# Two projections of the next block moved forward in the cross stage of a three-layer decoder kernel

## What is computed

```python
# linear attention, chunks of 32 keys (here as masked scores over each sequence of 64)
q, k, v = silu(rms(x) @ Wq.T), silu(rms(x) @ Wk.T), silu(rms(x) @ Wv.T)
g = sigmoid(rms(x) @ Wg.T)
x1 = layernorm(x + (linear_attention(q, k, v) * g) @ Wp.T)
# cross attention over a latent context of 64 channels, 16 heads
scores = (rope(q_big(x1)) @ W_qr) . (rope(ctx) @ W_kr)
ctx_c  = softmax(scores) @ rope(ctx)
x2 = layernorm(x1 + (ctx_c @ w_kc_kv) @ Wo.T)
# 32 experts of 96 hidden units, the best 8 of each token, weighted
out = layernorm(x2 + sum_e c_e * (silu(x2 @ Wg_e.T) * (x2 @ Wu_e.T)) @ Wd_e.T)
```

## Time and profile before

| | |
|---|---|
| Median of 3 runs | 843.66 us (843.52 to 843.76) |
| The profiled execution, device time | 843.54 us |
| Its span in the profile | 841.7 us |
| TensorE (PE) matmuls busy | 821.1 us, 98% |
| TensorE weight loads (PEld) busy | 658.0 us, 78% |
| VectorE (DVE) busy | 631.0 us, 75% |
| ScalarE (ACT) busy | 290.7 us, 35% |
| GpSimd (POOL) busy | 180.8 us, 21% |

### The profile page before, as it was taken

One profiled execution on the slowest core, in us unless ns is written; L12 is line 12 of the kernel. 1 busy time (PEld: TensorE's weight loads), 2 busy tenths in 40 slices (PEclk: granted clock), 3 DMA queues, 4 the chain that ended last, 5 costly groups with the idle time before them and its releaser, 6 DMA issues.

```text
span 841.7 us, 16104 instructions
## 1 busy us (share of the span) xinstructions
PE 821.1 (98%) x6386; PEld 658.0 (78%) x6386; DVE 631.0 (75%) x1392; ACT 290.7 (35%) x532; POOL 180.8 (21%) x156
## 2 busy tenths in 40 slices
PE   8999999999999999999999999999999999999996
PEld 6977677776887768776777788888888888888885
DVE  5587698899889998887957966666665666576576
ACT  5431263204432145303544423342323333232242
POOL 3046500663006630176312102100000000000121
PEclk9999999999999999999999999999999999999998
DMA  9300000100001000010220042102012021000001
GB/s 349 145 26 2 3 2 4 60 2 5 2 14 51 3 5 2 17 66 5 81 62 26 1 139 89 70 1 70 31 45 69 0 93 36 26 1 1 0 34 67
DMA packets 13092, 35.86 MB, mean 43 GB/s; under 512 B 1504, under 2 KB 2784, under 8 KB 12640
## 3 DMA queue, kind: packets, MB, share of 16 engines
q1 hardware_dynamic: 13024, 34.92, 12.1%
HBM read 30.26 MB, written 2.36 MB: 39 GB/s over the span
## 4 chain that ended last, share of the span: by engine, by line
PE 49%; DVE 2%; issue 1%; ACT 0%; POOL 0%; ACTq 0%; DVEq 0%
PE ps L259 15%; PE ps L260 15%; PE ps L261 15%; PE ps L1711 2%; PE ps L642 1%; PE ps L1702 0%; PE ps L1677 0%; PE ps L645 0%; PE ps L670 0%; DVE h_lo L374 0%; POOL roped L824 0%; ACT roped L979 0%; DVE su L543 0%; PE ps L1698 0%; PE ps L1542 0%
## 5 line engine op out<-in xcount | busy, mean ns | idle before, releaser
L824 POOL TENSOR_TENSOR roped<-prod 128x512 f32<-128x512 f32 x96 | 121.3, 1289 | 226.2 <-DVE prod L1175 226.1
L543 DVE TENSOR_TENSOR su<-sg,ps 128x512 f32<-128x512 f32 x96 | 66.0, 687 | 119.5 <-PE ps L261 117.3
L259 PE MATMUL ps<-y_hi,f_hi 128*128 128x512 f32 x384 | 150.8, 393 | 0.0
L261 PE MATMUL ps<-y_hi,f_lo 128*128 128x512 f32 x384 | 149.5, 389 | 0.0
L260 PE MATMUL ps<-y_lo,f_hi 128*128 128x512 f32 x384 | 149.4, 389 | 0.0
L403 ACT ACTIVATE sg<-ps 128x512 f32<-128x512 f32 x96 | 57.4, 598 | 249.1 <-PE ps L261 249.0
L1175 DVE TENSOR_TENSOR prod<-ps,ropeq 128x512 f32<-128x512 f32 x192 | 118.7, 682 | 21.7 <-PE ps L261 16.9
L259 PEld LDWEIGHTS ps<-y_hi,f_hi 128*128 128x128 f32 x384 | 72.1, 188 | 15.9 <-issue 1.1
L261 PEld LDWEIGHTS ps<-y_hi,f_lo 128*128 128x128 f32 x384 | 72.1, 188 | 15.0
L260 PEld LDWEIGHTS ps<-y_lo,f_hi 128*128 128x128 f32 x384 | 72.1, 188 | 14.9 <-issue 0.2
L259 PE MATMUL ps<-xT_hi,a_hi 128*128 128x512 f32 x192 | 79.2, 413 | 2.1 <-DVE prod L1175 2.1
(11 more groups left out here) (192 smaller groups left out, 1330.4 us busy)
## 6 DMA issues: line engine op xcount, KB each, us to landing
cb<-routing SPq DMA_DIRECT2D x32, 256.0 KB
f_raw<-in_L_ffn_gate_up_proj SPq DMA_DIRECT2D x8, 768.0 KB, 6.6
f_raw<-in_L_ffn_down_proj SPq DMA_DIRECT2D x8, 384.0 KB, 7.0
xb<-in_x SPq DMA_DIRECT2D x4, 512.0 KB, 4.1
lq<-in_L_xattn_Wq SPq DMA_DIRECT2D x1, 2048.0 KB, 14.3
x2T_all<-in_L_xattn_Wo SPq DMA_DIRECT2D x1, 2048.0 KB, 11.9
x2T_all<-x2T SPq DMA_DIRECT2D x4, 512.0 KB, 3.4
roped<-in_L_xattn_w_kc_q SPq DMA_DIRECT2D x1, 1536.0 KB, 10.0
```

What stands on the lines that cost most here:

```text
L259: pe.matmul(dst, l_hi, r_hi, start=first, stop=False, skip_group_check=check)
L261: return pe.matmul(dst, l_lo, r_hi, start=False, stop=last, skip_group_check=check)
L543: dve.tensor_tensor(su[:, k % 2], sg[:, k % 2], bank(2 * (k % 2) + 1), ALU.mult).then_inc(s_su, 1)
L824: pool.tensor_tensor(roped[:, 2 * (t % 4) + k], made(2 * t + k)[:, 0], made(2 * t + k)[:, 1], ALU.add)\
```

## The change

All of it is in the stage `cross` with a following block.

- PSUM: projection 3 of the blocks after the first writes bank 4 instead of bank 7.
- TensorE: projection 3 stands before turn(0) instead of behind it, and so projections 4, 5 and 6 each stand one place earlier; project 1 stands before turn(2); turn(3) stands before the first x2 turn.
- ScalarE: tanh 3, 4 and 5 move forward with their projections, the exponentials of turn 3 stand before the copy of turn(2), the copy of turn(3) before that of the first x2 turn.
- VectorE: the silus are done in the order 0, 2, 3, then shift(1), then 1; silus 4 and 5 follow each one place earlier, before shift(2) and before residual2(0).
- Waits: projection 3 no longer waits for a silu. Projection 4 waits for one (silu 0, bank 6). `context(0)`, which overwrites banks 4 and 5, waits for three silus at its first half instead of two at its second.

```diff
-    p_bank = lambda b, i: 5 if b and i == 2 else 6 + i % 2
+    p_bank = lambda b, i: {2: 5, 3: 4}.get(i, 6 + i % 2) if b else 6 + i % 2
...
             if following:
                 expo(0)
-                tanh(n, 0)
-                tanh(n, 1)
-                tanh(n, 2)
+                for i in range(4):
+                    tanh(n, i)
                 turned(0)
-                tanh(n, 3)
+                tanh(n, 4)
                 expo(1)
                 context(0)
-                tanh(n, 4)
+                tanh(n, 5)
                 expo(2)
                 turned(1)
-                tanh(n, 5)
                 context(1)
                 tanh(n, 6)
                 tanh(n, 7)
+                expo(3)
                 turned(2)
-                expo(3)
                 context(2)
+                turned(3)
                 xout(0)
-                turned(3)
                 xout(1)
...
                 normalise(b, 0)
+                silu(n, 0)
+                silu(n, 2)
+                silu(n, 3)
+                shift(b, 1)
                 silu(n, 1)
-                silu(n, 2)
-                shift(b, 1)
-                silu(n, 0)
                 normalise(b, 1)
-                silu(n, 3)
+                silu(n, 4)
                 shift(b, 2)
-                silu(n, 4)
+                silu(n, 5)
                 residual2(b, 0, 4)
                 normalise(b, 2)
-                silu(n, 5)
                 norm2(b, 0)
                 shift(b, 3)
...
-            if b and i >= 3:
-                pe.wait_ge(s_pa, 6 * b + (1 if i == 3 else i - 1))
+            if b and i >= 4:
+                pe.wait_ge(s_pa, 6 * b + (1 if i == 4 else i - 1))
...
-                    if following and t == 0 and h == 1:
-                        pe.wait_ge(s_pa, 6 * n + 2)
+                    if following and t == 0 and h == 0:
+                        pe.wait_ge(s_pa, 6 * n + 3)
...
                 scores(b, 1)
+                projection(n, 3)
                 turn(0)
-                projection(n, 3)
+                projection(n, 4)
                 context(0)
                 scores(b, 2)
-                projection(n, 4)
+                projection(n, 5)
                 project(0)
                 turn(1)
-                projection(n, 5)
+                projection(n, 6)
                 context(1)
-                projection(n, 6)
                 scores(b, 3)
                 projection(n, 7)
+                project(1)
                 turn(2)
-                project(1)
                 self_scores(n)
                 context(2)
                 self_context(n, 0)
                 self_context(n, 1)
+                turn(3)
                 xout(0)
-                turn(3)
                 attn_out(n, 0)
                 attn_out(n, 1)
```

## The result

The changed kernel takes 838.78 us (median of 4 runs, 838.74 to 838.86) against 843.65 us of the kernel before in the same comparison: ratio 0.9943, 95% interval 0.9931 to 0.9954, or 4.87 us less. The forecast was 839.3, range 837.9 to 841.3. The span fell from 841.7 to 837.0 us.

A forecast was written before the change was run, and what follows sets the result against it. TensorE was taken to set the time: 2.44 us of waits per cross, less new waits of 0.32, 0.52 and 0.16, gives 1.44, or 4.3 in three crosses; from 843.66 to 839.3 us, range 837.9 to 841.3.

The forecast's parts named there:

- idle column: The profile's listed TensorE waits, 1.68 a cross; counting by them gives 0.68 a cross gained, 841.6 us, kept as slow end.
- stall at scores 2: New TensorE wait of 0.52 before scores 2, until shift(1), now behind three silus, ends its last subtraction.
- 0.08 and 0.16: Time lost in front of context(1): 0.08 in the kernel before, 0.16 in the new order, waiting for turned(1).
- the sum: Net gain per cross: 2.44 us of old waits less new ones of 0.32, 0.52 and 0.16, making 1.44.
- mis-sized term: TensorE from context(1) to project 1: context, scores 3 and projection 7 take 3.70, the old 5.20 less 1.50 for projection 6.
- stretch forecast at 7.26: TensorE's project 1, turn(2), self scores and context(2), said to hold the same work as before, 7.26 us.
- the tail: Self context to attention output: self context 1.86, turn(3) with x2 turn 1.15; attention output starts at 232.37 instead of 233.81.
- Moving expo(3) costs nothing: On ScalarE, the exponentials of turn 3 ahead of turned(2) cost nothing while VectorE's shift(3) ends at 226.23.
- small covers: Spare times at project 1, attention output, context(2) and self context; rival that they fail: 841.2 to 840.3 us, chance 0.20.
- 0.29 at project 1: Spare time between the end of context(1)'s copies, 221.81, and project 1's start, 222.10; no wait expected.
- VectorE is the real bound: Rival: VectorE's chain to 226.23 is unchanged, new stalls equal the old ones, nothing gained, 843.7 us; chance 0.08 (or no effect).
- slower case: Rival: shift(3) ends later and delays context(2) through expo(3) and turned(2); 847.1 us at 3 us late; chance 0.04.

The follow-up runs named there:

- turn(3) alone: The kernel before with only turn(3) and its copy moved ahead of the first x2 turn; 841.84 us, ratio 0.998.
- four-silu kernel: The changed kernel with silu 1 also ahead of shift(1), so four silus instead of three stand before it; 840.38 us, ratio 0.9961.
- last variant: Beyond the changed kernel: projections 3 and 4 ahead of turn(0), projection 5 ahead of context(0), silu 0 ahead of the first normalise, among other moves; 837.88 us, ratio 0.9931.

## Why the prediction was right

*What bounds the kernel, and how to count.* The choice of starts over the idle column was right. The idle column led to 841.6, and 838.78 was measured; turn(3) alone gave 0.60 a cross where the column has 0.38 and the starts 0.54.

*Turn(0), projection 4, context(0), scores 2.* With 1.40 taken off, the forecast starts are 204.61, 206.14 and 208.46; measured 204.58, 206.12 and 208.42. The stall at scores 2 for shift(1) came where it was named. The four-silu kernel showed its mechanism: 0.53 paid for 0.60.

*Turn(1) and context(1).* Forecast 217.00, measured 216.95, at the end of turn(1)'s copy in both. The 0.08 and 0.16 that the prediction called lost there are not all waiting: the four-silu kernel, with no wait there, still shows about 0.07. As it stood in both kernels, the sum is not touched by it.

*The mis-sized term.* "Context, scores 3 and projection 7 take 5.20 - 1.50 = 3.70": it took 3.46. Projection 6 held 1.59 in its place between the two tiled groups (218.82 to 220.41), not the 1.50 that was taken off, and with it gone context(1) takes 0.91 instead of 1.02 and scores 3 takes 1.04 instead of 1.09. A projection cannot be cut out of a row of groups at its length elsewhere, because what it separates then stands together, and the passage between two tiled groups is cheaper. Scores 3 next to context(1) in the kernel before, and apart in the changed one, show it in both directions. Against it, the stretch forecast at 7.26 took 7.34 (220.41 to 227.75), and the tail 2.97 instead of 3.01. The sum from scores 1 to the attention output is 1.69 instead of 1.44. That the second cross began 1.44 earlier, just as forecast, is luck: the first cross gave 1.56, and it began 0.12 later in this execution.

*"Moving expo(3) costs nothing".* Right, but half the story: the text priced the risk of moving it, and not of leaving it. Left where it was, with project 1 moved, it costs 3.7 us. The prediction also gave the swap of project 1 and turn(2) no price; together with the move of the exponentials it costs 0.14 a cross by the times (838.78 against 838.37).

*The rivals.* The small covers held: 0.2 at the attention output, 0.4 at context(2) and 0.24 at self context measure 0.20, 0.35 and 0.23. Only the 0.29 at project 1 shrank, to 0.04, since project 1 came earlier than laid out. "VectorE is the real bound" is wrong for this change, but VectorE is the next bound, as the last variant shows. The rule of the Trainium skill (Perfetto Trace Analysis, Identifying the Most-Contended Engine) names VectorE, by 44.56 busy of 50.80 against 38.88 of weight loads. That did not stop this change from bringing 4.87 us; VectorE limits the step after it. The room for this one was the 1.29 us that VectorE stood idle for project 1; in the changed kernel its timeline of this stage lists, from 198.07 to the end of the gated products, only the 0.16. The slower case did not occur.

*Not tried.* Whether bank 4 has a price of its own. Projection 3 takes 1.49 there (201.99 to 203.48) against 1.50 in bank 7, though ScalarE's tanh 2 read bank 5 in that time (three tanhs from 201.38 to 202.94), which leaves no room for one. The projections were not moved one at a time either, so how their 3.3 to 3.5 us divide among them is open.

## What to carry to other kernels

When one engine is nearly full, lay the new order on the clock by start-to-start times, and give every moved group the time it has with its new neighbours: in this kernel two groups of 64 x 64 tiles side by side were cheaper than the same two with a full-array group between. Follow each queue that the move touches to its next reader. A move that shortens one wait can lengthen another engine's queue: here projections ahead of the turn put one more silu of 0.60 in front of the shift, and the new stall was 0.50.

## What was not expected of the hardware

Where a projection stands next to 64 x 64 tiles, TensorE loses time beyond the matmuls themselves: its last step in front of them is 0.33 instead of the usual 0.23, its first behind them 0.34. The first step is nearly as long behind the full-array transposes of a turn, 0.31, so it does not belong to tiles alone. The tiled groups too are shorter side by side: 0.91 for context(1) instead of 1.02. Removing one such island of a projection brought 0.37 us a cross (842.51 against 843.63 us in all); putting one back cost 0.20 (839.39 against 838.78).
